# Turning the row maxima of a gated attention layer: VectorE in 32x32 blocks and four DMAs in place of TensorE, ScalarE and one DMA

## The chip, the core and the metric

The kernel runs on one core of a Trainium2 chip. A core has a matrix engine (TensorE, PE in the profile, with its weight loads as PEld), VectorE (DVE), ScalarE (ACT), GpSimd (POOL) and a queue of SyncE (SP) that here issues all DMAs. The engines run side by side, each in the order of its own instructions, and wait for one another through semaphores. The metric is the device time of one execution in microseconds (us), lower is better.

## What is computed

A gated cross-attention layer and a gated feed-forward layer over 16 batches of 512 tokens with 512 channels, all in float32. Cut to what matters here:

```
def xattn(Q, K, V, mask, ...):          # 16 heads of 32 channels, 512 tokens
    q, k, v = projections of layernorm(x), ctx, ctx
    scores = einsum('bhqd,bhkd->bhqk', q, k) * 32 ** -0.5
    scores = where(mask == 0, -inf, scores); scores = where(causal, scores, -inf)
    attn = softmax(scores, axis=-1)      # its maximum over k is what this change moves
    return einsum('bhqk,bhkd->bhqd', attn, v) merged @ Wo.T + bo
x = x + tanh(g_xattn) * xattn(layernorm(x), ctx, ctx, mask, ...)
x = x + tanh(g_ffn) * ffn(layernorm(x), W_r, W_k, W_v, mu_r, mu_k)
```

The softmax subtracts from each query's scores their maximum over the keys. The kernel does this inside a matmul: two rows that stand under the 32-channel parts of each query hold the negated maximum, as a high and a low part, and the keys have ones there.

## The kernel before

There are 256 heads over all batches (N = 256), taken one per *slot*: `for i in SLOTS: slot(i)` on each engine. Slot i of TensorE computes the scores of head i (`scores`, L1382, three steps c = 0, 1, 2 that take turns in two banks `score_ps`) and, three slots later (LAG = 3), the transposed and shifted scores of head u = i - 3 for the exponential (`probabilities`, L1406, also in three steps). Between them stand the pieces of the projections that the table WORK gives to each slot of a batch (s = i mod 16), and in every fourth slot the products of four heads with the values (`values`, L1425, and the sums L1430 and L1433).

VectorE reads each block of scores as it comes (`maximum`, L1038, four per head) and leaves the negated row maxima of a pair of heads in `least`, 128 queries of a block on the partitions and 2 x 4 columns (two heads, four blocks of queries). Behind the last one of the pair, in the odd slot i = 2q + 1, it splits them (`split_maxima(q)`): a copy (L1046), the high part (L1050) and the low part (L1052), 8 columns each. They must come to two rows (MAX_ROW = 98 and 99) of `q_stack`, 512 queries long for each head, so they have to be turned. Before, this takes three steps in the even slot i = 2q + 2: TensorE multiplies the 16 columns with the unit matrix (`turn_maxima`, L1391, into `sum_ps`), ScalarE copies the 16 x 128 result to `max_rows` (`copy_maxima`, L641), and SP issues one DMA of 16 rows of 512 bytes to the stack (`stack_maxima`, L336). TensorE waits for it in slot 2q + 3, at step 0 of `probabilities` of the first head of the pair (head 2q), by the semaphores `max_stacked`. There are 128 pairs.

What sets the order around this: all engines take the slots in the order of the program. TensorE's turning stands in slots with i mod 4 = 0 just ahead of `values`, and in slots with i mod 4 = 2 behind the slot's first piece of projections. ScalarE's copy stands first in its even slots. SP's queue does in slot i first `stack_maxima`, then loads and stores of x (L298, L342, L346) or of the context (L302), and then the DMAs that put the parts of queries and keys into the stacks: `stack_q` (L311, three DMAs per pair of heads) in slots 1 and 3 mod 4, `stack_k` (L320, three DMAs, and for the first half of a batch one more for the mask, L326) in slots 2 and 3 mod 4. `stack_k(i + 2)` thus stands right behind `stack_maxima` in slots with i mod 4 = 2.

Of the kernel before, what the change touches and what calls it, by code (L numbers as in the profile page):

```python
# [9 lines left out]
F32 = mybir.dt.float32  # L10
F32R = mybir.dt.float32r
# [35 lines left out]
def gated_layer(nc, x, ctxT, mask, g_xattn, wqT, bq, wkT, bk, wvT, bv, woT, bo, g_ffn, ffn_wT, mu_k, mu_r, x1, mask_bias, out):  # L47
# [22 lines left out]
    RING = 5  # L70
    assert T == 4 and K == 4 and HG == 4 and H == 16
# [11 lines left out]
    with ExitStack() as ctx:  # L83
        def sb(name, shape, dt=F32):
            return ctx.enter_context(nc.sbuf_tensor(name, shape, dt))
# [44 lines left out]
        ident_parts = sb("ident_parts", [P, P], F32R)  # L130
        split_max = sb("split_max", [P, 2 * PAIR * T], F32R)
        max_rows = sb("max_rows", [2 * PAIR * T, P])
# [25 lines left out]
        ident_ready = sem("ident_ready")  # L158
# [17 lines left out]
        scores_done, scores_read = sem("scores_done"), sem("scores_read")  # L176
        max_moved, max_high, max_split = sem("max_moved"), sem("max_high"), sem("max_split")
        max_turned, max_copied = sem("max_turned"), sem("max_copied")
# [106 lines left out]
        def _(sp):  # L285
# [43 lines left out]
            def stack_maxima(q):  # L329
                n, a = q // 2 % 2, q % 2  # L330
                sp.wait_ge(max_copied, q + 1)
                if q >= 4:
                    sp.wait_ge(probs_done, 3 * (2 * q - 6))
                else:
                    sp.wait_ge(stacks_set, 4)
                sp.dma_start(q_stack[n][MAX_ROW:MAX_ROW + 2, 2 * a:2 * a + 2, :].bitcast(F32)  # L336
                             .rearrange("r j (t p) -> r (j t) p", p=P), max_rows[:]).then_inc(max_stacked[n][a], 16)
# [104 lines left out]
        def _(pool):  # L442
# [108 lines left out]
            nc.gpsimd.memset(eps[:], LN_EPS).then_inc(eps_set, 1)  # L551
            pool.wait_ge(pool_const, 2)
# [37 lines left out]
        def _(act):  # L590
# [45 lines left out]

            def copy_maxima(q):
                act.wait_ge(max_turned, q + 1)
                if q > 0:
                    act.wait_ge(max_stacked[(q - 1) // 2 % 2][(q - 1) % 2], 16 * ((q - 1) // 4 + 1))  # L640
                nc.scalar.copy(max_rows[:], sum_ps[0:2 * PAIR * T, 0:P]).then_inc(max_copied, 1)  # L641
# [109 lines left out]
            def first(i, b, s):  # L751

                if 0 <= b < B and s == 12:
                    high_part_attn(K * b)
                if 2 <= i <= N and i % 2 == 0:
                    copy_maxima(i // 2 - 1)
# [137 lines left out]
            act.wait_ge(pool_const, 5)  # L894
            nc.scalar.copy(ident_parts[:], ident[:]).then_inc(ident_ready, 1)
# [102 lines left out]
        def _(dve):  # L998
# [43 lines left out]
            def split_maxima(q):  # L1042

                here = score_ps[(6 * q + 5) % 2][:, 0:PAIR * T]
                dve.wait_ge(scores_read, 2 * T * (q + 1))
                nc.vector.tensor_copy(here, least[:, q % 2, :]).then_inc(max_moved, 1)  # L1046
                dve.wait_ge(max_moved, q + 1)
                if q > 0:
                    dve.wait_ge(max_turned, q)
                nc.vector.tensor_copy(split_max[:, 0:PAIR * T], here).then_inc(max_high, 1)  # L1050
# [315 lines left out]
        def _(pe):  # L1366
# [19 lines left out]
            def turn_maxima(q):  # L1386
# [24 lines left out]
            def values(G):  # L1411
# [16 lines left out]
                pe.wait_ge(max_copied, min(2 * G + 4, N // 2))  # L1428
# [159 lines left out]
            def slot(i):  # L1588
# [7 lines left out]
                if 2 <= i <= N and i % HG == 0:  # L1596
                    turn_maxima(i // 2 - 1)
# [3 lines left out]
                if 2 <= i <= N and i % HG == 2:  # L1601
                    turn_maxima(i // 2 - 1)
# [25 lines left out]
            pe.wait_ge(ident_ready, 1)  # L1628
# [94 lines left out]
```

## Time and profile before

| what | value |
|---|---|
| median of 3 runs | 1899.47 us (1899.12 to 1901.95) |
| span of the profiled execution | 1900.3 us |
| TensorE busy | 1868.2 us (98%), 11136 matmuls |
| VectorE busy | 1307.8 us (69%) |
| ScalarE busy | 1094.9 us (58%) |
| GpSimd busy | 1168.8 us (62%) |
| DMA engines' mean busy share, queue 1 | 44.9% |

The span is from the first to the last instruction of one execution taken by the hardware profiler. A matmul's duration in it is modelled and overlaps the next one's, so that what a matmul takes on TensorE is read from one start to the next. The attention slots run from about 40 us to 1350 us, the rest of the feed-forward layer after them. One batch of 16 slots takes 81.2 us. An idle time of an engine is given with who ended it ("<-").

### The profile page before, as it was taken

What the parts mean: (1) busy time and instruction counts of PE and PEld (TensorE: products, weight loads), DVE (VectorE), ACT (ScalarE), POOL (GpSimd) and SP (SyncE); (2) the same over time, 40 slices, a digit from 0 to 9 for tenths busy, and PEclk for the clock granted to TensorE, in tenths of its full rate; (3) what the DMA queues carried; (4) which work ended last, traced back from release to release, by engine and by line L of the source; (5) the groups of instructions that cost most, each with busy time, mean ns of one, the idle gap of its engine ahead of it and who ended that gap; (6) DMA issues with size and microseconds to landing.
All of it is one profiled execution on the core that took longest, in us unless ns stands there. A gap on an engine that the chain in (4) does not pass through costs nothing.

```text
span 1900.3 us, 35387 instructions
## 1 busy us (share of the span) xinstructions
PE 1868.2 (98%) x11136; PEld 1471.2 (77%) x11136; DVE 1307.8 (69%) x3680; ACT 1094.9 (58%) x2107; POOL 1168.8 (62%) x1833
## 2 busy tenths in 40 slices
PE   6999999999999999999999999998999999999998
PEld 5677777777777777777777777776778888888887
DVE  6776767776776776767776776777576756657554
ACT  4655555555555655555555555656676656565662
POOL 2776777777777776777777777777543334234331
PEclk9999999999999999999999999998999999999999
DMA  7455465445545455464555545463332231322311
GB/s 219 104 132 127 128 160 125 120 125 138 152 111 141 121 138 131 114 165 119 121 130 132 154 116 135 121 161 100 112 111 89 84 117 67 110 91 77 103 65 67
DMA packets 129226, 229.70 MB, mean 121 GB/s; under 512 B 18800, under 2 KB 20848, under 8 KB 128272
## 3 DMA queue, kind: packets, MB, share of 16 engines
q1 hardware_dynamic: 129040, 227.43, 44.9%
q8 instruction: 91, 1.49, 0.4%
q14 instruction: 95, 0.78, 0.2%
HBM read 92.06 MB, written 33.59 MB: 66 GB/s over the span
## 4 chain that ended last, share of the span: by engine, by line
PE 95%; DVE 3%; issue 1%; DMA 1%; ACT 1%; SPq 0%; ACTq 0%; DVEq 0%
PE proj_ps L41 15%; PE proj_ps L42 15%; PE proj_ps L43 15%; PE score_ps L1382 10%; PE prob_ps L1406 8%; PE value_ps L1425 8%; PE score_ps L41 3%; PE score_ps L42 3%; PE score_ps L43 3%; PE sum_ps L1433 2%; PE sum_ps L41 1%; PE value_ps L41 1%; PE sum_ps L43 1%; PE sum_ps L42 1%; PE value_ps L43 1%; PE value_ps L42 1%
## 5 line engine op out<-in xcount | busy, mean ns | idle before, releaser
L1038 DVE CUSTOM_DVE_ANT_0 score_ps<-score_ps,causal 128x128 f32<-128x128 f32 (+3 forms) x1024 | 488.7, 504 | 291.1 <-PE score_ps L1382 290.9
L654 ACT ACTIVATE probs<-prob_ps 128x512 f32<-128x512 f32 (+1 forms) x768 | 396.0, 528 | 368.9 <-PE prob_ps L1406 184.2
L1382 PE MATMUL score_ps<-k_stack,q_stack 97*128 97x128 f32 (+3 forms) x1024 | 318.8, 352 | 5.5 <-DVE least L1038 4.3
L1406 PE MATMUL prob_ps<-q_stack,k_stack 100*128 100x512 f32 (+3 forms) x1024 | 279.9, 314 | 1.7 <-DMA q_stack<-max_rows 1.5
L459 POOL TENSOR_TENSOR prob_sum<-probs 128x384 f32<-128x384 f32 x256 | 260.1, 1016 | 0.0
L1382 PEld LDWEIGHTS score_ps<-k_stack,q_stack 97*128 97x128 f32 x1024 | 187.3, 189 | 76.2 <-issue 40.9
L527 POOL TENSOR_TENSOR kact<-square,kact 128x512 fp32r<-128x512 f32 x64 | 83.5, 1315 | 236.7 <-ACT kact L737 236.7
L462 POOL TENSOR_TENSOR prob_sum<-prob_sum,probs 128x256 f32<-128x256 f32 x256 | 198.2, 774 | 37.0 <-POOL prob_sum L459 0.4
L1406 PEld LDWEIGHTS prob_ps<-q_stack,k_stack 100*128 100x128 f32 x1024 | 191.7, 190 | 21.1 <-DMA q_stack<-max_rows 2.2
L448 POOL TENSOR_SCALAR_AFFINE_SELECT probs<-probs 128x256 f32<-128x256 f32 x256 | 104.9, 410 | 152.0 <-ACT probs L654 151.8
L452 POOL TENSOR_SCALAR_AFFINE_SELECT probs<-probs 128x256 f32<-128x256 f32 x256 | 106.6, 416 | 126.5 <-ACT probs L654 126.5
L1425 PE MATMUL value_ps<-probs,v 128*32 128x512 f32 (+3 forms) x2048 | 152.6, 439 | 0.0
L1038 DVE DVE_READ_ACCUMULATOR2_ANT least<- 128x1 f32 x1024 | 144.0, 141 | 0.0
L1119 DVE TENSOR_TENSOR square<-square 128x512 f32<-128x512 f32 x64 | 46.3, 725 | 131.0 <-ACT square L729 130.9
L465 POOL TENSOR_TENSOR prob_sum<-prob_sum,probs 128x128 f32<-128x128 f32 x256 | 123.8, 483 | 20.1
L1425 PEld LDWEIGHTS value_ps<-probs,v 128*32 128x32 f32 x2048 | 60.8, 110 | 92.4 <-issue 81.1
L1108 DVE SCALAR_TENSOR_TENSOR tiles<-xT_room_high,mu,tiles 128x512 f32<-128x512 f32 x128 | 95.3, 763 | 46.6 <-ACT tiles L709 44.1
L41 PE MATMUL proj_ps<-mix_k_high,ffn_wk_high 128*128 128x512 f32 x256 | 104.0, 406 | 2.8 <-DVE mix_k_low L1114 2.8
L41 PE MATMUL proj_ps<-cT_high,wk_high 128*128 128x512 f32 x256 | 102.9, 402 | 0.4 <-DVE wk_low L1085 0.4
L41 PE MATMUL proj_ps<-wv_high,cT_high 128*128 128x512 f32 x256 | 101.6, 397 | 1.6 <-DVE staged L1021 1.6
L41 PE MATMUL proj_ps<-xT_high,wq_high 128*128 128x512 f32 x256 | 101.3, 396 | 0.0
L42 PE MATMUL proj_ps<-cT_low,wk_high 128*128 128x512 f32 x256 | 101.2, 395 | 0.0
(172 smaller groups left out, 4776.2 us busy)
## 6 DMA issues: line engine op xcount, KB each, us to landing
k_stack<-staged SPq DMA_DIRECT2D x384, 128.0 KB
q_stack<-staged SPq DMA_DIRECT2D x384, 128.0 KB, 3.1
x_io<-in_x SPq DMA_DIRECT2D x16, 1024.0 KB, 7.8
x<-x_io SPq DMA_DIRECT2D x64, 256.0 KB, 3.0
res<-x SPq DMA_DIRECT2D x64, 256.0 KB, 3.6
out_x<-res SPq DMA_DIRECT2D x64, 256.0 KB, 2.0
tiles<-in_x SPq DMA_DIRECT2D x15, 1024.0 KB, 5.5
tiles<-in_ctxT SPq DMA_DIRECT2D x60, 256.0 KB, 4.0
```

Source lines behind the costliest of these rows:

```text
L41: nc.tensor.matmul(out, s_high, m_high, start=first and n == steps[0], stop=False)
L42: nc.tensor.matmul(out, s_high, m_low, start=False, stop=False)
L43: done = nc.tensor.matmul(out, s_low, m_high, start=False, stop=last and n == steps[-1])
L452: nc.gpsimd.affine_select(out=pair, in_=pair, compare_op=ALU.is_ge, fill=0.0, base=0, pattern=[[0, 2], [1, P]], channel_multiplier=-1).the ...
L459: nc.gpsimd.tensor_tensor(total, here[:, P:S], here[:, PT_AT[1]:PT_AT[1] + LATE], ALU.add).then_inc(summed, 1)
L462: nc.gpsimd.tensor_tensor(total[:, P:LATE], total[:, P:LATE], here[:, PT_AT[2]:PT_AT[2] + 2 * P], ALU.add).then_inc(summed, 1)
L465: nc.gpsimd.tensor_tensor(total[:, 2 * P:LATE], total[:, 2 * P:LATE], here[:, PT_AT[3]:PT_AT[3] + P], ALU.add).then_inc(summed, 1)
L654: nc.scalar.activation(probs[:, u % RING, lo:hi], prob_ps[(3 * u + c) % 2][:, 0:hi - lo], ACT.Exp, scale=SCALE).then_inc(exp_done, 1)
L1038: nc.vector.tensor_tensor_reduce(out=here, in0=here, in1=causal[:, LATE - P * t:S], scale=-1.0, scalar=3e38, op0=ALU.add, op1=ALU.min, acc ...
L1382: last = nc.tensor.matmul(here[:, at:at + P * (t + 1)], q_stack[n][0:MASK_ROW + 1, j, P * t:P * t + P], k_stack[n][0:MASK_ROW + 1, j, 0:P ...
L1406: last = nc.tensor.matmul(here[:, at:at + width], k_stack[n][0:ROWS, j, P * k:P * k + P], q_stack[n][0:ROWS, j, P * k:S], start=True, stop ...
L1425: nc.tensor.matmul(value_ps[DH * j:DH * j + DH, P * k:S], v[:, value_block(b, g), k, at:at + DH], probs[:, (HG * G + j) % RING, PT_AT[k]:P ...
```

## The change

VectorE's `split_maxima` gets a fourth instruction: it turns the 32 columns of `split_max` (16 with the parts, 16 that GpSimd sets to zero once at the start) in blocks of 32 x 32 into `max_blocks`. Block c holds, on partitions 32c to 32c + 15, the 16 rows of parts for the queries 32c to 32c + 31 of each block of 128. Four DMAs, each of 16 partitions and 128 bytes per row, take them to the stack. `turn_maxima`, `copy_maxima` and the unit matrix's copy `ident_parts` go, and with them TensorE's waits for `refined` (there) and for `max_copied` (in `values`). VectorE waits for the four DMAs of the pair before, before it turns again.

```
@@ stack_maxima (SP)
-                sp.wait_ge(max_copied, q + 1)
+                sp.wait_ge(max_turned, q + 1)
...
-                sp.dma_start(q_stack[n][MAX_ROW:MAX_ROW + 2, 2 * a:2 * a + 2, :].bitcast(F32)
-                             .rearrange("r j (t p) -> r (j t) p", p=P), max_rows[:]).then_inc(max_stacked[n][a], 16)
+                rows = q_stack[n][MAX_ROW:MAX_ROW + 2, 2 * a:2 * a + 2, :].bitcast(F32).rearrange(
+                    "r j (t c p) -> r (j t) c p", t=T, p=BLOCK)
+                for c in range(P // BLOCK):
+                    sp.dma_start(rows[:, :, c, :], max_blocks[BLOCK * c:BLOCK * c + 2 * PAIR * T, :]
+                                 ).then_inc(max_stacked[n][a], 16)
@@ copy_maxima (ScalarE), once per even slot
-                act.wait_ge(max_turned, q + 1)
-                if q > 0:
-                    act.wait_ge(max_stacked[(q - 1) // 2 % 2][(q - 1) % 2], 16 * ((q - 1) // 4 + 1))
-                nc.scalar.copy(max_rows[:], sum_ps[0:2 * PAIR * T, 0:P]).then_inc(max_copied, 1)
@@ split_maxima (VectorE)
                 nc.vector.tensor_tensor(split_max[:, PAIR * T:2 * PAIR * T], here, split_max[:, 0:PAIR * T].bitcast(F32),
                                         ALU.subtract).then_inc(max_split, 1)
+                dve.wait_ge(max_split, q + 1)
+                if q > 0:
+                    dve.wait_ge(max_stacked[(q - 1) // 2 % 2][(q - 1) % 2], 64 * ((q - 1) // 4 + 1))
+                nc.vector.transpose(max_blocks[:], split_max[:].bitcast(F32)).then_inc(max_turned, 1)
@@ turn_maxima (TensorE), once per even slot
-                pe.wait_ge(max_split, q + 1)
-                ended = (2 * q + 1 - VALUES) // HG + 1
-                if ended > 0:
-                    pe.wait_ge(refined, ended)
-                nc.tensor.matmul(sum_ps[0:2 * PAIR * T, 0:P], split_max[:], ident_parts[:], start=True, stop=True
-                                 ).then_inc(max_turned, 1)
@@ probabilities (TensorE)
-                    pe.wait_ge(max_stacked[n][j // 2], 16 * (G // 2 + 1))
+                    pe.wait_ge(max_stacked[n][j // 2], 64 * (G // 2 + 1))
@@ values (TensorE)
-                pe.wait_ge(max_copied, min(2 * G + 4, N // 2))
```

How it stands in the engines' order. TensorE in a slot with i mod 4 = 2, here an early one that has no projection ahead of the turning; before:

```order
L1406 MATMUL prob_ps<-q_stack,k_stack 128x512 [waits exp_done]
L1391 MATMUL sum_ps<-ident_parts,split_max 16x128 [waits max_split]
L1382 MATMUL score_ps<-k_stack,q_stack 128x384 [waits max_split,scores_read]
L1406 MATMUL prob_ps<-q_stack,k_stack 128x384 [waits exp_done]
L1406 MATMUL prob_ps<-q_stack,k_stack 128x128
```

and after (L1398 is L1406 of before):

```order
L1398 MATMUL prob_ps<-q_stack,k_stack 128x512 [waits exp_done]
L1382 MATMUL score_ps<-k_stack,q_stack 128x384 [waits max_split,scores_read]
L1398 MATMUL prob_ps<-q_stack,k_stack 128x384 [waits exp_done]
L1398 MATMUL prob_ps<-q_stack,k_stack 128x128
L1382 MATMUL score_ps<-k_stack,q_stack 128x512 [waits scores_read]
```

One matmul of 128 columns is gone and nothing else on TensorE moves. VectorE from the end of an odd slot into the next; before:

```order
L1046 COPY score_ps<-least 128x8 [waits scores_read]
L1050 CAST split_max<-score_ps 128x8 [waits max_turned,max_moved]
L1052 TENSOR_TENSOR split_max<-score_ps,split_max 128x8 [waits max_high]
L1038 ISA score_ps,least<-score_ps,causal 128x128 [waits scores_done]
L1038 ISA least 128x1
```

and after (lines 1040, 1046, 1048 and 1032 are 1046, 1050, 1052 and 1038 of before):

```order
L1040 COPY score_ps<-least 128x8 [waits scores_read]
L1046 CAST split_max<-score_ps 128x8 [waits max_turned,max_moved]
L1048 TENSOR_TENSOR split_max<-score_ps,split_max 128x8 [waits max_high]
L1053 STREAM_TRANSPOSE max_blocks<-split_max 128x32 [waits max_stacked0_0,max_split]
L1032 ISA score_ps,least<-score_ps,causal 128x128 [waits scores_done]
```

The turning stands between the low part and the next head's first block of scores. SP's queue in the slot with s = 0; before:

```order
L326 DMA k_stack0<-mask_bias 2x2x512
L336 DMA q_stack1<-max_rows 2x8x128 [waits probs_done,max_copied]
L298 DMA tiles<-in_x 128x4x512 [waits c_low]
L342 DMA x_io<-in_x 128x4x512
L311 DMA q_stack1<-staged 32x2x512 [waits probs_done,q_low]
```

and after:

```order
L326 DMA k_stack0<-mask_bias 2x2x512
L339 DMA q_stack1<-max_blocks 2x8x32 [waits probs_done,max_turned]
L339 DMA q_stack1<-max_blocks 2x8x32 x3
L298 DMA tiles<-in_x 128x4x512 [waits c_low]
L345 DMA x_io<-in_x 128x4x512
```

Four issues stand where one stood, at the same place in the queue.

## Rows read from the trace of the kernel before

**Rows 1.** The page's first part, busy time of each engine.

```profile
PE 1868.2 (98%) x11136; PEld 1471.2 (77%) x11136; DVE 1307.8 (69%) x3680; ACT 1094.9 (58%) x2107; POOL 1168.8 (62%) x1833
```

**Rows 2.** Busy us by stretch, with clock and DMA share: third batch, then first slots.

```profile
core 0: us, PE busy (x) PEld busy (x) DVE busy (x) ACT busy (x) POOL busy (x), PEclk, DMA share, GB/s
196.40:277.60 81.20, 81.20 (x538) 62.87 (x538) 58.36 (x192) 46.17 (x95) 59.98 (x96) 1.00 0.54 132
...
40.00:115.00 75.00, 70.27 (x435) 52.59 (x434) 53.30 (x184) 41.80 (x87) 48.57 (x83) 0.98 0.55 128
```

**Rows 3.** Timeline, a batch in mid-run, slot s = 2: start, us, what.

```profile
602.20 0.17 DVE L1046 COPY score_ps<-least 128x8 f32<-128x8 f32 x1
602.40 0.17 DVE L1050 CAST split_max<-score_ps 128x8 fp32r<-128x8 f32 x1
602.60 0.17 DVE L1052 TENSOR_TENSOR split_max<-score_ps,split_max 128x8 fp32r<-128x8 f32 x1
...
603.94 0.22 PE L1391 MATMUL sum_ps<-ident_parts,split_max 128*16 128x128 f32 x1
604.00 0.39 PE L1382 MATMUL score_ps<-k_stack,q_stack 97*128 97x384 f32 x1
...
604.20 0.25 ACT L641 COPY max_rows<-sum_ps 16x128 f32<-16x128 f32 x1 [0.60 <-PE sum_ps L1391]
...
604.48 0.65 SPq L336 DMA_DIRECT2D q_stack<-max_rows  x1
605.17 1.84 SPq L320 DMA_DIRECT2D k_stack<-staged  x3
...
607.07 0.19 PEld L1406 LDWEIGHTS prob_ps<-q_stack,k_stack 100*128 100x128 f32 x1
```

**Rows 4.** First batch, slot 6: timeline of VectorE, SP and weight loads.

```profile
56.86 0.17 DVE L1052 TENSOR_TENSOR split_max<-score_ps,split_max 128x8 fp32r<-128x8 f32 x1
...
58.09 0.65 SPq L336 DMA_DIRECT2D q_stack<-max_rows  x1
...
60.22 0.19 PEld L1406 LDWEIGHTS prob_ps<-q_stack,k_stack 100*128 100x128 f32 x1 [0.52 <-DMA q_stack<-max_rows]
```

**Rows 5.** First batch, slots 4 and 10, timeline of SP, VectorE and weight loads.

```profile
48.78 0.62 SPq L326 DMA_DIRECT2D k_stack<-mask_bias  x1
...
52.42 0.19 PEld L1406 LDWEIGHTS prob_ps<-q_stack,k_stack 100*128 100x128 f32 x1
...
74.30 0.17 DVE L1052 TENSOR_TENSOR split_max<-score_ps,split_max 128x8 fp32r<-128x8 f32 x1
...
77.99 0.19 PEld L1406 LDWEIGHTS prob_ps<-q_stack,k_stack 100*128 100x128 f32 x1
```

**Rows 6.** TensorE's timeline around `values`, slot 4 and the last one.

```profile
611.93 0.39 PE L1406 MATMUL prob_ps<-q_stack,k_stack 100*128 100x512 f32 x1
612.16 0.22 PE L1391 MATMUL sum_ps<-ident_parts,split_max 128*16 128x128 f32 x1
612.31 0.64 PE L1425 MATMUL value_ps<-probs,v 128*32 128x512 f32 x4
...
1350.30 0.39 PE L43 MATMUL score_ps<-ffn_wr_high,mix_r_low 128*128 128x512 f32 x1
1350.62 0.64 PE L1425 MATMUL value_ps<-probs,v 128*32 128x512 f32 x4
```

**Rows 7.** VectorE's blocks of 128 columns, grouped over the whole span.

```profile
L1038 DVE CUSTOM_DVE_ANT_0 score_ps<-score_ps,causal 128x128 f32<-128x128 f32 x256 | 75.3, 294 | 97.1 <-PE score_ps L1382 97.1
```

**Rows 8.** VectorE, slot 10 of a batch, and the score load that needs it.

```profile
237.10 0.14 DVE L1038 DVE_READ_ACCUMULATOR2_ANT least<- 128x1 f32 x1
...
237.73 0.19 PEld L1382 LDWEIGHTS score_ps<-k_stack,q_stack 97*128 97x128 f32 x1
```

**Rows 9.** DMA issues: what, count, KB each, median us from issue to landing.

```profile
x_io<-in_mask SPq DMA_DIRECT2D x1, 32.0 KB, 1.8
```

**Rows 10.** Issue of the maxima's DMA and the queries' DMA: ns min/median/max.

```profile
L336 SPq DMA_DIRECT2D q_stack<-max_rows x128: 616/650/664, 41.6 to 1335.3; - x128
...
L311 SPq DMA_DIRECT2D q_stack<-staged x384: 542/597/1792, 26.4 to 1299.2; - x192
```

**Rows 11.** A batch's slots 5 and 6 with a slow issue of the queries' DMAs.

```profile
620.83 3.11 SPq L311 DMA_DIRECT2D q_stack<-staged  x3
...
627.00 0.19 PEld L1406 LDWEIGHTS prob_ps<-q_stack,k_stack 100*128 100x128 f32 x1
```

More of the change, by code:

```diff
@@ L70, in gated_layer @@
     RING = 5
+    BLOCK = 32
     assert T == 4 and K == 4 and HG == 4 and H == 16
@@ L129, in gated_layer @@
         least = sb("least", [P, 2, PAIR * T])
-        ident_parts = sb("ident_parts", [P, P], F32R)
-        split_max = sb("split_max", [P, 2 * PAIR * T], F32R)
-        max_rows = sb("max_rows", [2 * PAIR * T, P])
+        split_max = sb("split_max", [P, BLOCK], F32R)
+        max_blocks = sb("max_blocks", [P, BLOCK])
         stats = sb("stats", [P, T, 6])
@@ L157, in gated_layer @@
         mask_loaded, mask_scaled, mask_stored = sem("mask_loaded"), sem("mask_scaled"), sem("mask_stored")
-        ident_ready = sem("ident_ready")
         pool_const, eps_set, stacks_set, bo_ready = sem("pool_const"), sem("eps_set"), sem("stacks_set"), sem("bo_ready")
@@ L176, in gated_layer @@
         scores_done, scores_read = sem("scores_done"), sem("scores_read")
+        max_cleared = sem("max_cleared")
         max_moved, max_high, max_split = sem("max_moved"), sem("max_high"), sem("max_split")
-        max_turned, max_copied = sem("max_turned"), sem("max_copied")
+        max_turned = sem("max_turned")
         max_stacked = [[sem(f"max_stacked{n}_{a}") for a in range(2)] for n in range(2)]
@@ L551, in _ @@
             nc.gpsimd.memset(eps[:], LN_EPS).then_inc(eps_set, 1)
+            nc.gpsimd.memset(split_max[:].bitcast(F32), 0.0).then_inc(max_cleared, 1)
             pool.wait_ge(pool_const, 2)
@@ L635, in copy_v @@
                                ).then_inc(v_copied, 1)
-            def copy_maxima(q):
-                act.wait_ge(max_turned, q + 1)
-                if q > 0:
-                    act.wait_ge(max_stacked[(q - 1) // 2 % 2][(q - 1) % 2], 16 * ((q - 1) // 4 + 1))
-                nc.scalar.copy(max_rows[:], sum_ps[0:2 * PAIR * T, 0:P]).then_inc(max_copied, 1)
             def high_part_c(b, k):
@@ L754, in first @@
                     high_part_attn(K * b)
-                if 2 <= i <= N and i % 2 == 0:
-                    copy_maxima(i // 2 - 1)
             def second(i, b, s):
@@ L893, in _ @@
             split_weights("v", 3)
-            act.wait_ge(pool_const, 5)
-            nc.scalar.copy(ident_parts[:], ident[:]).then_inc(ident_ready, 1)
             act.wait_ge(gate_loaded, 16)
@@ L1049, in split_maxima @@
                     dve.wait_ge(max_turned, q)
+                else:
+                    dve.wait_ge(max_cleared, 1)
                 nc.vector.tensor_copy(split_max[:, 0:PAIR * T], here).then_inc(max_high, 1)
@@ L1384, in scores @@
                 last.then_inc(scores_done, 1)
-            def turn_maxima(q):
-                pe.wait_ge(max_split, q + 1)
-                ended = (2 * q + 1 - VALUES) // HG + 1
-                if ended > 0:
-                    pe.wait_ge(refined, ended)
-                nc.tensor.matmul(sum_ps[0:2 * PAIR * T, 0:P], split_max[:], ident_parts[:], start=True, stop=True
-                                 ).then_inc(max_turned, 1)
             def probabilities(u, c):
@@ L1595, in slot @@
                     probabilities(u, 0)
-                if 2 <= i <= N and i % HG == 0:
-                    turn_maxima(i // 2 - 1)
                 if i % HG == 0 and 0 <= i - VALUES < N:
@@ L1600, in slot @@
                 share(i, b, s, 0)
-                if 2 <= i <= N and i % HG == 2:
-                    turn_maxima(i // 2 - 1)
                 if now:
@@ L1627, in _ @@
                     project_v(0, m, k)
-            pe.wait_ge(ident_ready, 1)
             for k in range(2):
```

## The prediction

> **What bounds the kernel now.** I read the busy shares first: TensorE has 98% of the span and no other engine over 70% [rows 1]. Then the same by stretch. In a batch in mid-run TensorE is busy for 81.20 of 81.20 us, while VectorE, ScalarE and GpSimd have 20 us and more to spare; only the first batch (40 to 115 us) has some 5 us of idle TensorE [rows 2]. So a matmul taken from TensorE's row is worth what it takes there, work put on VectorE is worth nothing as long as nobody waits for it, and every new wait of TensorE costs its full length. The last question is where the maxima's path has slack, and for that I lay out one pair of heads in the timeline from the split to the weight load that waits for it [rows 3], and the first batch, where it was already late [rows 4, 5].
>
> **What goes: 128 matmuls and 128 ScalarE copies.** The turning's own duration of 0.22 us is modelled and overlaps what follows; what it takes is the time from its start to the next start: 603.94 to 604.00, 0.06 us [rows 3]. Ahead of `values` it looks dearer, 612.16 to 612.31, 0.15 us. But the first matmul of `values` also comes late without it: at the end of the slots it starts 0.32 us after a 512-column matmul (1350.30 to 1350.62), and with the turning between them it is 611.93 to 612.31, 0.38 us [rows 6]. The difference is 0.06 us again. So the gain is 128 x 0.06 = 7.7 us. The copy on ScalarE (0.25 us and a wait of 0.60 us for the matmul [rows 3]) lies on an engine that TensorE does not wait for in mid-run [rows 2]: its absence makes exponentials start earlier and is worth 0 by itself. Only where the maxima's path ends late does it count, and it is in the next sum.
>
> **What comes on VectorE: 128 turnings.** No row shows one. The nearest are the 8-column instructions just ahead of it, 0.17 us each and 0.20 us from start to start when each waits for the one before [rows 3], and a 128-column one at 0.294 us [rows 7]. 32 columns lie near the small end: I take 0.18 us, between 0.17 and 0.30, plus the 0.03 us between dependent instructions. VectorE is thus some 0.2 us later at the next head's first block. Who waits for that is TensorE, which writes the score banks again. In slot 2 the next read is followed by further ones and slack is ample; the tightest place I found in mid-run is slot 10, where VectorE's read ends at 237.24 and the load that needs it starts at 237.73: 0.49 us become 0.29, still hidden [rows 8]. The cover is gone only in the first batch; I put 0.3 us there, in the sum for it. Also behind the turning wait the low parts of keys that SP sends on; they have the same slack of a slot or more.
>
> **What becomes of the maxima's path.** This is the term that decides. Before, in slot 2 [rows 3]: the split ends at 602.77, TensorE turns it only at 603.94, the DMA is issued at 604.48, and the weight load that needs it starts at 607.07, without a wait. How long does the DMA take to land? One place shows it: issued at 58.09, and it releases the load at 60.22, 2.13 us later [rows 4]; the shortest landing in the list of DMA issues is 1.8 us [rows 9]. I take the middle, 1.97 us. So it lands at 606.45, with 0.6 us to spare. After: turned at 602.77 + 0.03 + 0.18 = 602.98, first issue 603.01. The issue takes 0.65 us, never over 0.664 [rows 10], and the next DMA starts 0.69 us after it (604.48 to 605.17 [rows 3]). The fourth is therefore issued at 603.01 + 3 x 0.69 = 605.08 and lands at 607.05. The load wants it at 607.07 - 0.06 = 607.01. It is 0.04 us late: **four issues in a row eat all that the shorter path gives.** With the bounds: issues 0.62 us apart (the keys' three DMAs take 1.84 us [rows 3]), turning in 0.17, landing in 1.8 gives 606.66, 0.35 us early; turning in 0.30 and landing in 2.13 gives 607.33, 0.32 us late. Slots 2 and 6 of each batch are alike in this; outside the first batch that is 30 places: 30 x 0.04 = 1.2 us, between 0 and 9.6 us. In the slots with i mod 4 = 0 `values` stands between, and the load comes over 2 us later; in slots 10 and 14 the turning stood later or the load does. They keep their slack.
>
> The rule on this of the Trainium skill, "DMA: Bandwidth & Descriptors": its section on the anatomy of one DMA gives a fixed cost of about 2.0 us that does not depend on size, which the row's 2.13 us agrees with, and by that each quarter lands no sooner than the whole did. The same page's specifications say that under 512 bytes per row the engines do a read-modify-write, which speaks against this change (rows go from 512 to 128 bytes); its section "Why small descriptors are slow (HBM only)" exempts copies within SBUF. No row here shows rows of 128 bytes. By the first the landing would be late by more than I assume and the slower rival below holds, by the second nothing changes.
>
> **The first batch** has no output projections, so its slots are shorter, and the path had no slack. Slot 6: the split ends at 57.03, so the first issue is at 57.27, the fourth at 59.34, landing (2.13 here) 61.47, against 60.22 [rows 4]: 1.2 us. Slot 4: SP is busy until 49.40, first issue 49.43, fourth 51.50, landing 53.47 against 52.42 - 0.06: 1.1 us [rows 5]. Slot 10: split ends 74.47, fourth issue 76.78, landing 78.75 against 77.93: 0.8 us [rows 5]. The three DMAs more per pair also push the keys' DMAs behind them, some 0.2 us that these waits don't cover already, and VectorE 0.3 us: 3.6 us together, between 2.5 and 5.
>
> **Irregular places.** Now and then an issue takes long, up to 1.79 us [rows 10]. In slots 5 and 6 at 620 us SP is busy until 623.94; four issues from there put the landing at 623.97 + 2.07 + 1.97 = 628.01, against 627.00 - 0.06: 1.1 us late, where one DMA was in time [rows 11]. I count about five such places of 0.3 to 1.1 us, and 384 more issues on SP bring a few more: 2.5 us, between 0.5 and 5.
>
> **The sum**: -7.7 + 0 + 1.2 + 3.6 + 2.5 = -0.4 us, against the profiled execution's 1900.3 us. That execution is 0.8 us over the median of the runs, so against the median: 1899.1 us. A measurement of this kernel can tell a change of about 0.2%, 3.8 us, from none; this is none. Ends: -7.7 + 0 + 2.5 + 0.5 = -4.7 and, with all high, -7.7 + 9.6 + 5 + 5 = +11.9.
>
> **Rivals.** (a) **The turning's time is simply won.** The issues follow one another at 0.62 us, or the landing is nearer 1.8: slots 2 and 6 keep 0.2 us or more of slack, the first batch and the irregular places cost their lower ends: -7.7 + 0 + 2.5 + 0.5 = -4.7, that is 1894.8. For it speaks TensorE's full row [rows 2]; against it that no issue of this DMA was under 0.616 us [rows 10]. (b) **The four DMAs set the pace: slower.** The place is the load of `probabilities` in slots 3 and 7. It decides from 607.01 on: each 0.1 us beyond costs 30 x 0.1 = 3 us. With 0.32 us late there (the upper bound, or rows of 128 bytes that land 0.25 us later), 9.6 instead of 1.2: +8.0, 1907.5; the same delay adds in the first batch. For it speaks that I find zero slack, so every underestimate counts; against it that the trace shows only one landing above 2 us, in the busy first batch. (c) **VectorE becomes the bound.** Its price would be 0.3 us for each turning at slot 10 and near it, only if one took over 0.5 us, nearly twice the 128-column row [rows 7]: 16 x 0.3 = 5 us more, 1904. (d) That it doesn't do what it says: the order shows the 128 matmuls gone and nothing moved, so this has no share.
>
> **Chances.** Within 0.2%: 0.46, the sum above. Faster by over 0.2% (rival a): 0.27. Slower by over 0.2%: 0.27, of which rival b 0.23 and rival c 0.04. The range: 1893.5 (a with small losses) to 1907 (b short of its worst), which leaves some 2 in 10 outside. The likeliest case's own range is 1896 to 1903.
>
> **What would show it.** TensorE's wait list should get a row of `probabilities` loads that wait for the DMA from `max_blocks`: about 3 us from the first batch, up to 3 us of single long ones, and in slots 3 and 7 either many tiny ones (my case), none (a) or 30 of 0.2 us and more (b). The mid-run batch of 81.2 us should become 80.7 plus these waits. SP's issues should stand 0.69 us apart; the turning should take 0.17 to 0.3 us. I am wrong if TensorE's start-to-start times elsewhere change, or if the keys' or queries' loads start to wait in mid-run, for which I allowed nothing.

## The result, and the profile after

The changed kernel takes 1909.71 us (median of 5 runs, 1906.47 to 1910.23) against 1900.33 us for the kernel before beside it; the ratio is 1.0039, with a 95% interval from 1.0027 to 1.0052. By the ratio the change makes the kernel **slower by about 7.4 us**, 0.39%; the two medians alone lie 9.4 us apart. The forecast was 1899.1 us and no measurable change, its range ended at 1907.0: sign and size are wrong. The kernel before has medians from 1900.33 to 1903.57 us beside the runs below, so ratios are used from here on. One of its five runs here took 3062.62 us, and the ratio goes by the others.

The page of the changed kernel, its first part (as [rows 1]) and a part of its fourth, the shares of the chain that ended last:

```profile
PE 1867.3 (98%) x11008; PEld 1468.7 (77%) x11008; DVE 1321.1 (69%) x3808; ACT 1071.4 (56%) x1978; POOL 1171.5 (61%) x1834
...
PE 87%; SPq 5%; DVE 4%; DMA 2%; issue 1%; ACT 1%; ACTq 0%; DVEq 0%
```

TensorE has its 128 matmuls less, and the same share. What is new is SP's queue with 5% of the chain that sets the end; before it had 0%, and TensorE 95%.

**Where the time went** is seen with a mark that both traces have: the start of `values` in the first slot of the second batch (slot 16 of all), and that in slot 8 of the last batch. Timeline of TensorE, before and then after (start, us, what):

```profile
105.27 2.36 PE L1425 MATMUL value_ps<-probs,v 128*32 128x512 f32 x32
...
1282.55 2.36 PE L1425 MATMUL value_ps<-probs,v 128*32 128x512 f32 x32
```

```profile
111.36 2.36 PE L1417 MATMUL value_ps<-probs,v 128*32 128x512 f32 x32
...
1290.98 2.36 PE L1417 MATMUL value_ps<-probs,v 128*32 128x512 f32 x32
```

The first batch loses 6.1 us, the 14.5 batches after it 8.4 - 6.1 = 2.3 us, and the rest gives 1.9 us back (the spans are 1906.8 and 1900.3), for which no run shows a cause; in a second profile of the same kernel, below, the rest gives 0.5 us back. Below, each kernel is measured with these two marks.

**The first batch.** TensorE's wait lists there, after, from 40 to 117 us (waited for: us in total, times, longest), then the busy times from 40 us to the first mark, after and before (columns as in [rows 2]):

```profile
PE prob_ps L1398 <- DMA q_stack<-max_blocks: 3.2, 3, 1.8
PE score_ps L1382 <- DVE least L1032: 2.5, 5, 1.0
PE score_ps L1382 <- DMA k_stack<-staged: 1.7, 1, 1.7
```

```profile
40.00:111.36 71.36, 62.96 (x346) 47.20 (x345) 48.78 (x172) 35.77 (x70) 43.23 (x74) 0.90 0.49 102
```

```profile
40.00:105.27 65.27, 60.54 (x355) 45.63 (x354) 47.18 (x165) 37.02 (x77) 43.20 (x74) 0.97 0.53 112
```

Idle time went from 65.27 - 60.54 = 4.73 us to 71.36 - 62.96 = 8.40 us: 3.7 us more waiting. But with nine matmuls less TensorE was also *busy* for 2.4 us longer, and the last columns say why: the mean granted clock fell from 0.97 to 0.90. After the waits TensorE ran at the lower of its two levels, 1.2 instead of 2.4 GHz, for 6.8 us from 62 us and for 6.8 us from 86 us; before there was one such stretch, 3.4 us from 83 us. The second profile of the changed kernel has 10.2 us at the lower level and parts the loss otherwise: 4.3 us more waiting than before and 1.5 us more work. That the fall follows from the waits is read from where it stands; no experiment parts the two. One stretch of each kind of after (granted clock in the third column from the right), and `values` in slot 12, at half clock, which at full clock takes 2.36 us as above:

```profile
62.00:69.00 7.00, 5.79 (x19) 4.59 (x23) 2.74 (x13) 2.93 (x6) 3.92 (x6) 0.51 0.73 139
...
93.00:100.00 7.00, 7.00 (x40) 5.63 (x33) 5.06 (x15) 5.06 (x10) 4.92 (x6) 1.00 0.11 32
```

```profile
87.77 4.50 PE L1417 MATMUL value_ps<-probs,v 128*32 128x512 f32 x32
```

The chain of waits of after names who made TensorE wait (pieces in order of time: start, us, what). It runs for over 12 us on SP alone:

```profile
39.61 0.60 SPq L311
40.31 0.65 SPq L339
...
42.99 0.59 SPq L320
...
47.50 0.60 SPq L320
...
51.57 0.61 SPq L339
52.22 1.65 DMA q_stack<-max_blocks
53.91 0.50 PE prob_ps L1398
...
57.27 0.59 SPq L311
...
61.52 1.64 DMA q_stack<-max_blocks
63.20 0.80 PE prob_ps L1398
```

From 39.61 to 52.22 us one issue follows another: the maxima (L339), keys (L320), the mask (L326), queries (L311), keys and maxima again. The load in slot 4, at 52.42 in [rows 5], can't start before 52.22 + 1.65 = 53.87. In slot 6 the queries' three issues stand ahead of the maxima's four, and the load comes at 63.20 instead of 60.22 [rows 4].

**In mid-run** the weight loads' waits of after (117 to 1290 us) are these; before, the same stretch had 0.3 us of the first kind, once, and none of the two others. The matmuls themselves waited less for the maxima there, 4.1 us in seven places, but start by start the loss follows the weight loads' list: 2.3 us between the marks against -5.4 with one DMA (below) is 7.7 us.

```profile
PEld prob_ps L1398 <- DMA q_stack<-max_blocks: 7.3, 12, 1.4
PEld proj_ps L41 <- DVE staged L1021: 4.4, 14, 0.3
PEld proj_ps L41 <- DVE attn_low L1073: 2.5, 11, 0.2
```

Slot 2 of a batch without such a wait, as in [rows 3], timeline of after:

```profile
528.41 0.21 DVE L1053 STREAM_TRANSPOSE max_blocks<-split_max 128x32 f32<-128x32 f32 x1
528.65 2.64 SPq L339 DMA_DIRECT2D q_stack<-max_blocks  x4
...
532.56 0.19 PEld L1398 LDWEIGHTS prob_ps<-q_stack,k_stack 100*128 100x128 f32 x1
```

The fourth issue starts 2.03 us after the first, at 530.68, and 1.64 us later, at 532.32, the maxima are there: 0.24 us before the load. So the four issues do fit. Where they don't is mostly where SP is busy when the maxima are ready. Of the twelve waits of the first kind five belong to the maxima of slot 12 (3.7 us), four to those of slot 4 (2.4 us), where the mask, queries and keys stand ahead, and three to those of slot 2 (1.2 us). In slot 12 the next batch's loads stand ahead of them:

```profile
166.89 2.75 SPq L302 DMA_DIRECT2D tiles<-in_ctxT  x3
169.75 1.86 SPq L311 DMA_DIRECT2D q_stack<-staged  x3
170.30 0.21 DVE L1053 STREAM_TRANSPOSE max_blocks<-split_max 128x32 f32<-128x32 f32 x1
171.65 1.99 SPq L320 DMA_DIRECT2D k_stack<-staged  x3
173.74 2.66 SPq L339 DMA_DIRECT2D q_stack<-max_blocks  x4
177.67 0.19 PEld L1398 LDWEIGHTS prob_ps<-q_stack,k_stack 100*128 100x128 f32 x1 [0.78 <-DMA q_stack<-max_blocks]
```

Turned at 170.5, the maxima are issued from 173.74 on, and the weight load waits 0.78 us.

### The profile page after: what moved, and what is told of

The parts are those of the page before. It is cut to its first block, busy times and chain, and to the rows that moved or that the text cites. A ratio compares the mean times of both kernels' runs of the same rounds, so it can differ in the third digit from the quotient of the medians.

```text
span 1906.8 us, 35391 instructions
## 1 busy us (share of the span) xinstructions
PE 1867.3 (98%) x11008; PEld 1468.7 (77%) x11008; DVE 1321.1 (69%) x3808; ACT 1071.4 (56%) x1978; POOL 1171.5 (61%) x1834
## 4 chain that ended last, share of the span: by engine, by line
PE 87%; SPq 5%; DVE 4%; DMA 2%; issue 1%; ACT 1%; ACTq 0%; DVEq 0%
PE proj_ps L41 14%; PE proj_ps L42 14%; PE proj_ps L43 14%; PE score_ps L1382 8%; PE prob_ps L1398 7%; PE value_ps L1417 7%; PE score_ps L41 3%; PE score_ps L43 3%; PE score_ps L42 3%; PE sum_ps L1424 2%; SPq L339 2%; SPq L320 1%; PE value_ps L41 1%; PE value_ps L43 1%; PE sum_ps L43 1%; PE value_ps L42 1%
## 5 line engine op out<-in xcount | busy, mean ns | idle before, releaser
L652 ACT ACTIVATE probs<-prob_ps 128x512 f32<-128x512 f32 (+1 forms) x768 | 401.2, 530 | 454.2 <-PE prob_ps L1398 232.9
L1398 PE MATMUL prob_ps<-q_stack,k_stack 100*128 100x512 f32 (+3 forms) x1024 | 282.9, 317 | 11.4 <-DMA q_stack<-max_blocks 10.5
L1398 PEld LDWEIGHTS prob_ps<-q_stack,k_stack 100*128 100x128 f32 x1024 | 192.6, 191 | 34.9 <-DMA q_stack<-max_blocks 14.5
L468 POOL TENSOR_TENSOR prob_sum<-prob_sum,probs 128x128 f32<-128x128 f32 x256 | 129.3, 505 | 20.1
```

What stands on the lines that cost most here:

```text
L468: nc.gpsimd.tensor_tensor(total[:, 2 * P:LATE], total[:, 2 * P:LATE], here[:, PT_AT[3]:PT_AT[3] + P], ALU.add).then_inc(summed, 1)
L652: nc.scalar.activation(probs[:, u % RING, lo:hi], prob_ps[(3 * u + c) % 2][:, 0:hi - lo], ACT.Exp, scale=SCALE).then_inc(exp_done, 1)
```

## Experiments

The theory: what costs is the number of issues, by a longer path of the maxima and by SP's queue, most of it in the first batch. The rivals: VectorE's turning, and a gain of 7.7 us that isn't there. Each ratio has 5 or more runs of its kernel, but four of before with its DMA in four; "marks" are the starts of `values` in one profiled run against 105.27 and 1282.55 us of before, the second with the first taken off.

| kernel | ratio to before (95%) | first mark | between the marks |
|---|---|---|---|
| changed kernel | 1.0039 (1.0027 to 1.0052) | +6.1 | +2.3 |
| changed kernel, again | 1.0040 (1.0027 to 1.0053) | +5.8 | +0.3 |
| one of four DMAs | 0.9957 (0.9945 to 0.9970) | -1.9 | -5.4 |
| one and three idle ones | 1.0003 (0.9994 to 1.0012) | +1.9 | -3.2 |
| four in the first batch, one later | 1.0002 (0.9993 to 1.0010) | +5.7 | -4.9 |
| before, with a turning on VectorE | 1.0002 (0.9993 to 1.0011) | -0.6 | +2.6 |
| changed, with a matmul | 1.0057 (1.0044 to 1.0069) | +6.7 | +8.5 |
| before, its DMA in four | 1.0444 (1.0428 to 1.0460) | +9.1 | +74.4 |
| keys behind the maxima | 1.0112 (1.0092 to 1.0133) | +1.2 | +26.7 |
| keys behind, in three slots | 0.9998 (0.9989 to 1.0006) | +2.4 | -3.4 |
| before, keys in three slots | 0.9997 (0.9988 to 1.0005) | -1.6 | +0.2 |
| two queues | 0.9994 (0.9985 to 1.0002) | +2.3 | -5.2 |
| two queues, keys behind | 1.0009 (1.0000 to 1.0017) | -2.1 | -1.2 |
| two queues, keys in three slots | 0.9986 (0.9977 to 0.9995) | -0.3 | -4.9 |
| two queues, keys in the first batch | 0.9983 (0.9974 to 0.9992) | -0.2 | -4.7 |

**The changed kernel again**, beside the kernels with the keys behind the maxima and with two queues.

> The changed kernel once more, beside the others of this job, since the kernel before took 1903.6 us in the last one against 1900.3 us at first: the ratio should again be 1.004 (1.003 to 1.005). It is what the next three are compared with.

1908.38 us, ratio 1.0040: the result stands. The marks of this second profile show the spread of single profiles: 0.3 us between the marks where the first had 2.3. A difference of 2 us between two profiles is therefore no finding by itself.

**One of the four DMAs alone:**

```
-                for c in range(P // BLOCK):
-                    sp.dma_start(rows[:, :, c, :], max_blocks[BLOCK * c:...]).then_inc(max_stacked[n][a], 16)
+                sp.dma_start(rows[:, :, 0, :], max_blocks[0:2 * PAIR * T, :]).then_inc(max_stacked[n][a], 16)
```

> The changed kernel with only the first of the four DMAs per pair (the numbers of queries 32 and up of each block stay at their start value, so three quarters of the maxima are left out). Theory A, the four issues in a row on SP cost the time: the path is 2.03 us shorter and SP has 384 issues less, so the waits of the first batch, its stretches at half clock and the long waits in mid-run go; what is left is the won matmuls (-7.7 us) and VectorE's later releases of banks (15 + 11 short waits, 7 us of idle weight loads at most, some 4 us): 1896 to 1898 us. Theory B, VectorE's fourth instruction costs the time: stays at 1905 or more.

1895.77 us against 1903.57 us beside it, 7.8 us faster. The three further issues cost 1.0039 - 0.9957 = 0.0082, about 15.6 us. No wait of a load for the maxima is left in mid-run, and the first batch runs at full clock (0.90 in after):

```profile
40.00:103.39 63.39, 57.41 (x345) 43.84 (x345) 48.42 (x172) 35.72 (x70) 43.36 (x74) 1.00 0.57 116
```

It also shows that the matmuls' gain is there: with the turning on VectorE and one DMA, nearly all of the 7.7 us is won.

**One real DMA, and three of the same shape behind it** that fetch zeros into tiles nobody reads:

```
+                for c in range(1, P // BLOCK):
+                    if q > 0:
+                        sp.wait_ge(extra_stored[c - 1], 16 * q)
+                    sp.dma_start(spare[c - 1][:], fixed[BLOCK * c:...]).then_inc(extra_stored[c - 1], 16)
```

> As the run with one DMA (three quarters of the maxima are left out), but SP issues three DMAs of the same shape behind it, to tiles that nobody reads. TensorE waits for the first alone. It splits theory A: if the length of the maxima's own path is what costs (the fourth lands 2.03 us after the first), this is as fast as the run with one DMA, 1896 to 1898 us; if the occupied queue costs, which sends keys, queries and the next maxima later, it is as slow as the changed kernel, 1906 to 1910 us. I expect the queue to matter in the first batch and in slot 12, where SP is behind: 1900 to 1903 us.

Ratio 1.0003. SP is as busy as in the changed kernel, but the maxima's path is as short as with one DMA. So the occupied queue costs 1.0003 - 0.9957 = 0.0046, 8.7 us, and the longer path 1.0039 - 1.0003 = 0.0036, 6.9 us. By their intervals each is known to some 3 us, so both matter, and which is the larger is open. In the first batch (40 to 117 us) the wait is now at the keys, whose issues stand behind the idle ones, and the maxima cost little:

```profile
PE score_ps L1390 <- DMA k_stack<-staged: 2.0, 1, 2.0
...
PE prob_ps L1406 <- DMA q_stack<-max_blocks: 0.4, 1, 0.4
```

**Four DMAs in the first batch, one in all others:**

```
-                for c in range(P // BLOCK):
+                for c in range(P // BLOCK if q < 8 else 1):
```

> The changed kernel with all four DMAs per pair in the first batch (pairs 0 to 7) and only the first of the four after it (three quarters of the maxima are left out there). It parts the 15 us between the changed kernel and the run with one DMA: by the traces, TensorE is 6.2 us behind the kernel before at the end of the first batch with four and 1.8 us ahead with one, so this run should be 8 us over the run with one DMA (0.996): 1.000 of the kernel before (0.9985 to 1.001). The other 7 us are then what the four issues cost in mid-run. If the first batch were made up later, 0.996 to 0.997.

Ratio 1.0002. Against one DMA everywhere, the first batch's 24 issues cost 0.0045, 8.6 us, and by the remainder the 360 others 7.0 us: **about half of what the issues cost comes from one batch of sixteen.** Each of the two parts is again known to some 3 us. Its waits there are those of after:

```profile
PE prob_ps L1401 <- DMA q_stack<-max_blocks: 3.1, 3, 1.7
PE score_ps L1385 <- DMA k_stack<-staged: 1.6, 1, 1.6
```

**Before, with the turning's work added on VectorE** (32 columns of zeros into a tile of its own, at the place where the changed kernel turns):

```
+                    dve.wait_ge(extra_done, q)
+                nc.vector.transpose(extra[:], zeros[:]).then_inc(extra_done, 1)
```

> The kernel before with VectorE's fourth instruction added (a 32-column turning of a tile of zeros into one that nobody reads, same place, same wait for the instruction ahead); TensorE's turning, ScalarE's copy and the one DMA stay. It measures VectorE's price alone. Theory A: the low parts of keys and of the attention output come 0.24 us later in slots 10 and 14, TensorE waits there for the bank or the low part, 0.3 us per batch: +3 to +5 us. Theory B: +8 us or more. My prediction had 0.3 us.

Ratio 1.0002: 0.4 us, between -1.3 and +2.1, by the times, and 2.6 us between the marks. The trace has a cause for these: at the end of slot 10 of a batch a weight load waits for VectorE's low part, as in after:

```profile
PEld proj_ps L41 <- DVE staged L1031: 2.9, 14, 0.2
```

So VectorE's turning costs something between 0 and 3 us. That it makes the loss is excluded.

**The changed kernel with a matmul** of the old one's shape where the turning stood, which nobody waits for:

```
+                nc.tensor.matmul(sum_ps[0:2 * PAIR * T, 0:P], ident_parts[:, 0:2 * PAIR * T], ident_parts[:], ...)
```

> The changed kernel with a matmul of 16 x 128 columns added to TensorE where the turning stood (its result is not read; the unit matrix is its input, so it waits for no maxima). It measures what the matmul takes: 128 x 0.06 = +7.7 us over the changed kernel if TensorE's row is full; less, down to +4 us, if the waits that the change brought would swallow it.

Ratio 1.0057, 0.0017 over the changed kernel's: 3.3 us, with intervals that leave 0 to 6.5 us, less than 7.7. The profile of this run spans 1916.3 us, 9.5 us more. In the traces of before and after, start by start, TensorE gains 0.06 us at each place where a turning stood. Between the marks stand 116 of these matmuls, 7.0 us by that price, and this run is there 6.2 us behind the first profile of the changed kernel and 8.2 us behind the second. So the marks agree with the price, while the times alone don't settle it. The kernel with one DMA, 7.8 us faster than before, speaks for it too.

**Before, with its one DMA cut into four** of 16 rows x 128 bytes; the matmul and the copy stay:

```
-                sp.dma_start(... .rearrange("r j (t p) -> r (j t) p", p=P), max_rows[:])...
+                for c in range(4):
+                    sp.dma_start(rows[:, :, c, :], max_rows[:, 32 * c:32 * c + 32]).then_inc(max_stacked[n][a], 16)
```

> The kernel before with its one DMA per pair cut into four of 32 queries each (16 rows of 128 bytes); TensorE's turning and ScalarE's copy stay. It asks what four DMAs cost without the earlier start that VectorE's turning gives. From the traces the fourth is issued 2.03 us after the first and lands 1.65 us after its issue, against 1.92 us for the one of 512-byte rows: the maxima land 1.76 us later. Slots 2, 6 and 14 of each batch had 0.68 us to spare, so 1.08 us are missing in 45 places of mid-run: +49 us; the first batch adds some 8 us. 1950 to 1965 us, ratio 1.026 to 1.034. If TensorE's waits there were absorbed by slack behind them, less than +20 us.

1988.35 us against 1902.12: 86 us, of which the text above had counted 57. The places counted were as computed: start by start, slots 2, 6 and 14 lose 1.0 to 1.1 us each. What was missed is mostly slot 12, where in 14 of the 15 later batches a weight load waits 0.2 to 2.3 us, with the same queue of loads ahead as in after. Its waits (117 to 1350 us):

```profile
PE prob_ps L1408 <- DMA q_stack<-max_rows: 53.2, 55, 2.1
```

This is what the four DMAs cost where the path isn't shortened on VectorE. The two halves of the change don't add up: the four DMAs cost 86 us alone, and with VectorE's turning 15.6 us.

**The keys behind the maxima.** In slots 3 mod 4 SP issues queries and keys, and the maxima of the next slot stand behind. Here the keys' DMAs come after the maxima's:

```
                 if 2 <= i <= N and i % 2 == 0:
                     stack_maxima(i // 2 - 1)
+                if i % HG == 0 and 0 < i and i + 2 < N:
+                    stack_k(i + 2)
...
-                    stack_k(i + 3)
```

> The changed kernel with one piece of SP's queue moved: in slots 3 mod 4 the three or four DMAs of the next pair's keys (used three slots later) stand no longer ahead of the maxima's DMAs of the following slot but right behind them. If SP's place in its queue is what makes the maxima late in slots 0 mod 4 (in slot 12 the first issue is 2.29 us behind the turning in the median), slots 4, 8 and 12 lose their waits: 3 to 5 us under the changed kernel. If the length of the four issues alone counts, no change (within 1 us).

A miss: 1.0112, slower than the change itself. The maxima of slots 4, 8, 12 are in time, but those of slot 2 are late, and the chain shows that it isn't SP: four issues 0.65 us apart, and then 4.39 us for the landing.

```profile
199.41 0.65 SPq L339
200.10 0.64 SPq L339
200.78 0.61 SPq L339
201.43 4.39 DMA q_stack<-max_blocks
```

```profile
PE prob_ps L1399 <- DMA q_stack<-max_blocks: 18.5, 18, 2.6
```

The loads of x, 1 MB each, which SP issues in slots 0 and 1, come later by the keys' issues, and the 8 KB of maxima travel behind them: the DMA engines are busy for 0.75 of these 4.39 us, against 0.02 in the 1.64 us from 61.52 us in after. The waits of 18.5 us are not the whole of the 26.7 us between the marks; behind four of the five longest of them TensorE's granted clock was at its lower level for 3.4 us each time. I took from this that the keys may move in slots 4, 8 and 12 only:

```
+                if s in (4, 8, 12) and i + 2 < N:
+                    stack_k(i + 2)
...
-                    stack_k(i + 3)
+                    if s == 15:
+                        stack_k(i + 3)
```

> The changed kernel with the next pair's keys behind the maxima in slots 4, 8 and 12 of each batch, but not in slot 0. In the run that moved them in all four, the maxima of slot 2 landed 2.65 us after their last issue in the median (1.65 before the move) and up to 4.5, since the megabyte loads of slots 0 and 1 were issued later and were still in the DMA queues; slots 4, 8 and 12 had lost their waits. By that reading this run keeps the good half: ratio to the kernel before 0.998 to 1.001 (the changed kernel has 1.004). If moving keys is bad in itself, over 1.006.

1903.53 us, ratio 0.9998. That is 0.0042 under the changed kernel's 1.0040: the order of SP's queue alone makes up for the whole loss, with all 512 issues in place. It also bears out that the landing in slot 2 was held up by the loads of x, since slot 0 is all that was left as it was. The same order in the kernel before, as a control:

> The kernel before with the keys moved in slots 4, 8 and 12 of each batch: a control for the two above. TensorE waits for no maxima in mid-run there, so only the waits of the first batch can go: ratio 0.999 to 1.000. If it is as fast as the run with two queues and the move, the gain is the move's and not the change's.

0.9997 (0.9988 to 1.0005): nothing, since with one DMA the maxima had slack. The order is worth something only together with the four issues.

**Two queues:** ScalarE issues the last two of the four, at the place where its copy stood, SP the first two.

```
+            def stack_half(q):
...
+                for c in range(2, 4):
+                    nc.scalar.dma_start(rows[:, :, c, :], max_blocks[BLOCK * c:...]).then_inc(max_stacked[n][a], 16)
```

> The changed kernel with the third and fourth DMA of each pair issued by ScalarE, first in its even slots, instead of by SP. The path gets 1.3 us shorter and SP has 256 issues less; ScalarE's row gets two issues of 0.6 us in place of the copy of before. By theory A (four issues in a row, half path and half queue) some 10 of the 15 us between the changed kernel and the one with one DMA come back: 1.004 becomes 0.998 (0.996 to 1.000) of the kernel before. If ScalarE's later exponentials hold up TensorE instead, it stays over 1.002.

Ratio 0.9994, 0.0046 or 8.7 us under the changed kernel beside it. In mid-run no matmul waits for the maxima any more; what is left there is VectorE, beside the first batch (+2.3 us at the first mark):

```profile
PEld proj_ps L41 <- DVE staged L1036: 4.8, 14, 0.3
PEld proj_ps L41 <- DVE attn_low L1088: 3.8, 15, 0.3
```

The marks leave out the last slots, and there this kernel gives back what it won: it is 2.9 us ahead of before at the second mark, and its span is before's, 1900.3 us. From 1290 to 1356 us two matmuls wait for the maxima, where before has one wait of 1.2 us:

```profile
PE prob_ps L1413 <- DMA q_stack<-max_blocks: 4.3, 2, 2.2
```

The three combinations of two queues with a moved order, everywhere, in slots 4, 8 and 12, and in the first batch only:

> Both of the two moves. If they remove different waits, 0.996 of the kernel before, as the run with one DMA; it would be the version that keeps what the change wins. If ScalarE holds up TensorE, over 1.000.

> The same move, with the third and fourth DMA of each pair on ScalarE's queue. The waits of the first batch go (that run with all four moves was 2 us ahead of the kernel before at the end of the first batch, and lost it later in slots 2 to 4), and a batch gains the 0.3 us of the run with two queues: -2 - 15 x 0.3 = -6.5 us, ratio 0.9965 (0.995 to 0.998).

> Two queues, and the keys moved in the first batch alone (slots 4, 8, 12). As the run before it if only the first batch needs the move: ratio 0.9965 (0.995 to 0.998).

1.0009, 0.9986 and 0.9983. The first repeats the lesson of slot 0. The two others hit the sign but not the size, which I had put at 0.9965: at the second mark they are 5.2 and 4.9 us ahead of before, near the 6.5 us expected, but their spans only 1.5 and 3.3 us, with 4.2 and 4.1 us of waits for the maxima in the last slots. The last takes 1899.15 us against 1902.94 beside it and is about 3.2 us faster than before (0.9974 to 0.9992). **These two beat both kernels.** Against the kernel before with the keys moved in three slots (0.9997), which has the same order as the first of the two, the lead of 0.0011 is within the intervals. The last one's first batch takes what before took, at before's clock:

```profile
40.00:105.12 65.12, 58.88 (x345) 45.15 (x343) 48.38 (x172) 36.22 (x69) 43.47 (x74) 0.97 0.52 113
```

Not tried: all maxima in one or two DMAs from the blocks of 32 rows, and a queue on GpSimd.

## Why the prediction was wrong, point by point

The sum was -7.7 + 0 + 1.2 + 3.6 + 2.5 = -0.4 us. The profiles differ by +6.5 us, the times by +7.4.

**The matmuls, -7.7: right.** Each is worth 0.06 us start by start, the kernel with one DMA is 7.8 us faster, and the added matmul costs 6.2 to 8.2 us between the marks. By the times of that experiment alone the total is not settled (0 to 6.5 us).

**Slots 2 and 6, 1.2: too high, by the landing.** Issues were 2.03 us from the first to the fourth (2.07 assumed), the turning took 0.211 us (0.18 assumed), and the landing 1.64 us (1.97 assumed). The landing had been the middle between 1.8 and 2.13 us of rows with other shapes. So the maxima came 0.2 us early instead of 0.04 late, which was rival (a): in slot 6 no load waited for them, and in slot 2 three did, which the irregular places below take in. Rival (b)'s mechanism, the four DMAs setting the pace, was the true one, but neither in slots 3 and 7 nor by the landing: four issues fit into the slack only where SP stands ready.

**The first batch, 3.6: this step failed, by what it left out.** The waits were of the size given, 3.7 us more idle time. But it took SP as free once the maxima were turned. In slot 4 it went by the end of a row of before (49.40), which the three further issues of the pair ahead push to 50.20, and the load was 1.5 us late for 1.1. In slot 6 it let the first issue start at 57.27, while SP, already before, had the queries' issues in hand until 57.63; the row of SP's timeline was there to be read:

```profile
55.78 1.85 SPq L311 DMA_DIRECT2D q_stack<-staged  x3
```

By that load TensorE was 63.20 - 60.22 = 3.0 us late, where 1.1 + 1.2 had been counted, and the scores of slot 12 waited 1.7 us for the keys behind the four issues, against 0.7 before. What was missing altogether is that TensorE, having waited, ran at 1.2 GHz for 13.6 us instead of 3.4: that is the second part of the loss, 62.96 us of work for which the kernel with one DMA, at full clock, needs 57.41. The term measured 6.1 us by the marks, and 6.6 without the 0.5 us of won matmuls in it, against 3.6.

**Irregular places, 2.5: too small.** Nine of the twelve waits, 6.1 of 7.3 us, fall on slots 4 and 12, where SP has a queue ahead of the maxima: mask, queries and keys, or the next batch's loads and then queries and keys. The prediction said of the slots with i mod 4 = 0 that the load comes over 2 us later and kept them out of the sum, without asking when SP gets to them. There are also the slow issues it spoke of, such as this one in slot 2, where three queries took 2.84 instead of 1.87 us:

```profile
608.49 2.84 SPq L311 DMA_DIRECT2D q_stack<-staged  x3
611.42 2.64 SPq L339 DMA_DIRECT2D q_stack<-max_blocks  x4
...
615.13 0.19 PEld L1398 LDWEIGHTS prob_ps<-q_stack,k_stack 100*128 100x128 f32 x1 [0.55 <-DMA q_stack<-max_blocks]
```

Together they are 7.3 us in mid-run, by the weight loads' list of waits; the second profile has 5.9 us.

**VectorE, 0: too small.** Only the score banks had been looked at [rows 8]. The keys' low part, which I had given "the slack of a slot or more", is what a projection's weight load waits for at the end of slot 10, some 0.2 us in each batch, and the low part of the attention, for which a load waits at the end of slot 6, adds less than 0.1. That is 2 to 3 us by the traces, and less than 2.1 us by the times.

**The terms as measured** give -7.7 + 6.6 + 7.3 + 1.6 = +7.8 us, against 6.5 by the profiles and 7.4 by the times; the slots after the second mark are left out, and the 1.6 us for VectorE are an estimate, from the kernel with one DMA, which gains 5.4 us between the marks where 116 matmuls are worth 7.0.

**The base** is no part of the error. The prediction held the profiled execution's span against a median of whole times, and a span is shorter than its own run's time (1906.8 against 1908.59 us in after); but only the difference of -0.4 us was carried over to the median.

**The rule on small rows** was put rightly as undecided. The rows show 1.64 us from the last issue to the landing for 128-byte rows. The landing of 512-byte rows shows in three places of before, not in one as the prediction has it: 2.08 us in the busy first batch, 1.9 us from 1275.38 us on, and 4.2 us in the last slots. The fixed cost of about 2.0 us, which the prediction takes from the Trainium skill, "DMA: Bandwidth & Descriptors", stands there for DMAs that GpSimd issues; SP's small copies took 1.64 us here. Of the Trainium skill, "DMA: Bandwidth & Descriptors", the section "Why small descriptors are slow (HBM only)", which exempts copies within SBUF, is what the trace agrees with; no run shows a cost of the read-modify-write under 512 bytes that its specifications name.

## What to carry to other kernels

Replacing one DMA by four is not a matter of one path's length: lay out the issuing engine's whole queue for the densest stretch, because every transfer behind it moves too; here that queue was about half of the cost, and either reordering it or using a second queue brought the kernel back to the time of before. Look at the densest stretch first (a prologue or first batch without filler work), since about half of the cost fell on a sixteenth of the slots, and count a wait of TensorE there as more than its length when the granted clock falls after it. And before a small DMA is moved, see which bulk loads it then travels behind.

## What the runs showed of the hardware that was not expected

- TensorE's clock: after waits of up to 1.8 us in the first batch it was granted half its clock for 6.8 us, twice (in a second profile for 6.8 and 3.4 us); with fewer issues (one DMA) the same stretch had a clock of 1.00. `values` took 4.50 instead of 2.36 us.
- Small copies within SBUF of 16 rows x 128 bytes land 1.64 us after the start of their issue while the DMA engines' busy share is 0.02, and in 4.39 us behind loads of 1 MB, at a share of 0.75.
- SP starts a DMA of this kind mostly 0.65 to 0.70 us after the one before (once 0.92), and twenty issues, of maxima, keys, masks and queries, stood back to back, their starts spread over 12.6 us.
- VectorE's turning of 128x32 took 0.211 us, between the 8-column and the 128-column rows.
